# Local attention, six layers on one core: weighing the values ahead of projecting new ones on TensorE, and copying the new values out last on ScalarE

## The reference

```python
qkv = x @ Wqkv                      # x: tokens shifted by one in half of the channels
q, k, v = split(qkv)
q = rotary(l2norm(q) * qs);  k = rotary(l2norm(k) * ksc)
sim = einsum('bhwie,bhwje->bhwij', q, k_of_this_and_previous_window) * 8.0
sim = where(mask, -max, sim)        # windows of 32 tokens, each sees 64 keys
attn = softmax(sim)
out = einsum('bhwij,bhwje->bhwie', attn, v_of_this_and_previous_window)
x = out @ Wo + x
x = ffn(shift_tokens(x)) + x
```

## Time and profile before

| what | value |
|---|---|
| median of three runs | 4894.09 us |
| profiled execution | 4860.85 us, span 4859.0 us |
| the six layers | from about 1619 us to 4859 us of the span |
| steps of one tile | 32 in a layer, 192 in all, plus three draining steps in a layer |
| TensorE busy, whole span | 91% |
| VectorE, ScalarE, GpSimd busy | 76%, 57%, 45% |

### The profile page before, as it was taken

How to read it: one execution, slowest core, us unless ns; L and a number is a source line. 1 busy time by engine, 2 the same in 40 slices (tenths; PEclk the granted TensorE clock), 3 DMA queues, 4 the chain that set the end, 5 groups by cost and what they waited for, 6 DMA issues and landing times. The chain is left out here.

```text
span 4859.0 us, 169452 instructions
## 1 busy us (share of the span) xinstructions
PE 4413.6 (91%) x75386; PEld 2749.0 (57%) x75386; DVE 3699.8 (76%) x4213; ACT 2755.6 (57%) x3767; POOL 2167.2 (45%) x1739
## 2 busy tenths in 40 slices
PE   7959997767998699999999999999999999999998
PEld 5623333543333376756776577646775667657674
DVE  5668884137886588858987799868996888869885
ACT  4527775334777366545665566555665565556564
POOL 4340000330000466636664566636663666546661
PEclk9979998887999899999999999999999999999999
DMA  1021111112111211111111111111111111211110
GB/s 43 8 78 28 45 44 45 52 52 61 42 41 32 63 42 42 38 44 39 42 39 49 37 38 42 38 45 42 38 42 41 42 42 38 59 28 38 42 38 27
DMA packets 109872, 204.69 MB, mean 42 GB/s; under 512 B 30514, under 2 KB 58802, under 8 KB 107314
## 3 DMA queue, kind: packets, MB, share of 16 engines
q1 hardware_dynamic: 107096, 189.65, 15.1%
q0 software_dynamic: 2048, 4.20, 0.3%
HBM read 67.52 MB, written 22.81 MB: 19 GB/s over the span
## 5 line engine op out<-in xcount | busy, mean ns | idle before, releaser
L2056 POOL TENSOR_TENSOR part_of_layer<-part_of_layer,sine_of_layer 128x512 f32<-128x512 f32 x768 | 963.4, 1276 | 612.1 <-DVE sine_of_layer L1932 612.1
L2067 POOL TENSOR_TENSOR part_of_layer<-part_of_layer,inverse_of_layer 128x1024 f32<-128x1024 f32 x384 | 730.5, 1902 | 259.8 <-ACT inverse_of_layer L1818 244.7
L980 ACT ACTIVATE prob_of_ca<-ps 128x1024 f32<-128x1024 f32 (+3 forms) x768 | 593.2, 813 | 245.9 <-PE ps L858 170.3
L1929 DVE TENSOR_TENSOR part_of_layer<-ps,rope 128x1024 f32<-128x1024 f32 x384 | 466.0, 1213 | 35.7 <-ACT square_of_layer L1806 34.0
L1932 DVE TENSOR_TENSOR sine_of_layer<-ps,rope 128x1024 f32<-128x1024 f32 x384 | 464.7, 1210 | 0.0
L1849 ACT ACTIVATE values_of_layer<-ps 128x1024 f32<-128x1024 f32 x192 | 196.6, 1024 | 450.0 <-PE ps L1692 450.0
L876 PE MATMUL ps<-keys_of_ca,queries_of_ca 64*128 64x512 bf16 (+3 forms) x1536 | 326.1, 342 | 117.4 <-DVE top_of_ca L1013 59.7
L1711 PEld LDWEIGHTS ps<-prob_t_of_layer,mixed_of_layer 64*64 64x64 f32 x12288 | 340.1, 134 | 161.2 <-issue 157.9
L1718 PE MATMUL ps<-heads_out_of_layer,wo 128*128 128x128 f32 x3072 | 413.1, 278 | 11.7 <-ACT heads_out_of_layer L1838 10.3
L1968 DVE TENSOR_REDUCE total_of_layer<-prob_of_layer 128x16 f32<-128x1024 f32 x192 | 234.2, 1220 | 232.8 <-ACT prob_of_layer L1842 232.8
L1618 PE MATMUL ps<-qkv,shifted 128*128 128x512 f32 x768 | 382.2, 620 | 25.0 <-POOL values_of_layer L2070 19.9
(11 more groups left out here) (238 smaller groups left out, 8774.8 us busy)
## 6 DMA issues: line engine op xcount, KB each, us to landing
mixed_of_layer<-values_of_layer SPq DMA_DIRECT2D x636, 128.0 KB
mixed_of_layer<-values_of_layer SPq DMA_DIRECT2D x264, 64.0 KB
queries_of_ca<-q_parts SPq DMA_DIRECT2D x384, 32.0 KB
keys_of_ca<-k_parts SPq DMA_DIRECT2D x384, 32.0 KB
qkv<-in_qkv SPq DMA_DIRECT2D x6, 1536.0 KB, 6.4
q_parts<-parts_of_ci SPq DMA_DIRECT2D x16, 384.0 KB, 2.5
k_parts<-parts_of_ci SPq DMA_DIRECT2D x16, 384.0 KB, 2.6
rope<-in_rope SPq DMA_DIRECT2D x6, 1024.0 KB, 9.0
```

What stands on the lines that cost most here:

```text
L980: nc.scalar.activation(prob[:, i % 2, 2 * two:2 * two + 2, j:], ps[:, 2 * two:2 * two + 2, j:], ACT.Exp, scale=scale).then_inc(raised, 1)
L1929: nc.vector.tensor_tensor(part[:, t % 2, side], by_head(slot), table(2 * side, t), ALU.mult).then_inc(parts, 1)
L2056: nc.gpsimd.tensor_tensor(out, out, sine[:, side, :, (1 - to) * half:(2 - to) * half], ALU.add).then_inc(rotated, 1)
L2067: nc.gpsimd.tensor_tensor(part[:, t % 2, side], part[:, t % 2, side], by, ALU.mult).then_inc(scaled, 1)
```

## The change

In TensorE's list `weigh` of tile n-2 is called before `make_v` of tile n; in ScalarE's list `out_v` of tile n moves from before `raise_p` to behind `out_o`. Nothing is added or removed, and no wait is edited: each function takes its waits along.

```diff
@@ TensorE
                     steps((make_next_q, 0), (make_k, 0), (turn_q, 1), (project, 3), (turn_k, 1), (turn_last_p, 2),
-                          (project_rest, 3), (turn_other_p, 2), (last(lambda: turn(1)), 2), (score, 1), (last(lambda: turn(0)), 1), (make_v, 0), (weigh, 2),
+                          (project_rest, 3), (turn_other_p, 2), (last(lambda: turn(1)), 2), (score, 1), (last(lambda: turn(0)), 1), (weigh, 2), (make_v, 0),
                           (last(lambda: turn(2)), 2), (last(lambda: back(0)), 2))
@@ ScalarE
                     steps((square_next_q, 0), (square_k, 0), (out_q, 1), (out_k, 1), (out_p, 2), (last(lambda: square_of(1)), 2), (invert, 0),
-                          (out_v, 0), (raise_p, 1), (last(lambda: square_of(0)), 1), (out_o, 2), (last(lambda: norm_invert(0)), 1), (shift_low, 4))
+                          (raise_p, 1), (last(lambda: square_of(0)), 1), (out_o, 2), (out_v, 0), (last(lambda: norm_invert(0)), 1), (shift_low, 4))
```

## The result

The changed kernel takes **5351.85 us** (median of 4 runs, 5320.29 to 5367.73) where the kernel before takes 4893.99 us (4 runs): a ratio of 1.0926, 95% interval 1.0886 to 1.0966. The profiled execution took 5346.37 us, 485.5 us more than the profiled one of before. The forecast of 5157 us had the sign, and its range ended at 5235 us: too low by 195 us of 458.

The account below looks back on a forecast made before the run. TensorE was taken to bound the step: 8.38 + 5.13 + 1.87 us plus 0.10 us for other gaps, 15.48 us against 14.06. Over 180 steps, with step 32, 263 us more: 5157 us, ends 5089 (widened to 5075) and 5235 us.

Parts of the forecast that it names:

- The block ends: Gaps inside weigh stand where TensorE passes into the next fetched block of 256 instructions, which isn't there yet.
- Point 1: TensorE from the step's start to the start of score: unchanged at 8.38 us.
- Point 2: score and weigh together: 3.42 us of work, 5.13 us with the fetch; weigh's wait for VectorE's key reading costs nothing.
- Point 3: make_v on TensorE: 1.87 us as before, now with the next make_q behind it.
- the sum: Step of 15.48 us, 1.42 us over 14.06; 256 us in 180 steps, 263 us with step 32.
- Point 4: raise_p on ScalarE can start some 0.15 us earlier, worth nothing because TensorE has the longer loop.
- Point 5: out_v ends 16.5 us in, 1.1 us into the next step; turn_q, SyncE's DMAs and square_q stay covered.
- Point 6: In step 32, turn_q of tile 31 waits for make_v and out_v: 1.26 us more per layer, 7.6 us.
- The second case: Rival: the block is there in time, only weigh's wait moves; 14.2 us a step, 4929 us, 0.7% slower; chance 8%.
- The faster case: Rival: fetch runs far enough ahead, weigh loses its gaps; step 13.76 us, 4840 us; chance 3%.

Follow-up runs that it names:

- e4: Changed kernel with make_v's four matmuls done twice, once unused between score and weigh, once behind weigh: 5200.07 us, ratio 1.0672.
- e5: Changed kernel with the last four pairs of heads left out of weigh, 128 instructions instead of 256: 4962.29 us, ratio 1.0153.
- e3: Changed kernel with two of make_v's four matmuls put back between score and weigh: 5031.87 us, ratio 1.0324.
- e6: Kernel before with out_v behind out_o on ScalarE, but shift_low ahead of raise_p and the last tile's values copied out first: 4884.58 us, ratio 0.9993.
- e2: Kernel before with only ScalarE's half of the change, out_v behind raise_p and out_o: 4894.56 us, ratio 1.0046.
- e7: Kernel before with an added wait in weigh of tile n-2 for raise_p of tile n-1: 5683.02 us, ratio 1.1614.
- e1: Kernel before with only TensorE's half of the change, weigh ahead of make_v: 5574.55 us, ratio 1.1432.

## Why the prediction was right and wrong, point by point

**The block ends: right.** Gaps of 0.8 to 2.4 us, 1.5 on average from one weight load to the next, in 185 of 192 steps; e4 and e5 show that it is the spacing and the place of the block ends. With TensorE's instructions of the trace counted one by one, its semaphore instructions among them, all 185 gaps stand at a multiple of 256 from each other, to one instruction; so do the 26 of the kernel before and the 86 of e5. From the start of a block in `score` to the first instruction of the next one, in `weigh`, passed 3.5 us on average (1.1 us until the instruction packet started, 1.1 us for the packet, 1.4 us more until that instruction ran); in the two thirds of the steps where no other block end came just before, 3.39 us; step 32 of the kernel before had given 3.4 us on average over the six layers. One reading of the prediction was off without harm: the four transposes of step 32 are 8 instructions, four loads and four matmuls, and not 16.

```profile
3684.08 0.42 PEld L1738 LDWEIGHTS ps<-sb_ident,shifted 128*128 128x128 f32 x4
```

**Point 1, `make_q` to `score` 8.38 us: right** (8.37 us in the step shown).

**Point 2, the pair in 5.13 us: a little low.** 1.71 + 3.74 = 5.45 us. Step 32 of the kernel before doesn't have what a third of the steps have now, a block end that follows closely on another one; there the next block took 3.85 us to come. Another part is `weigh` itself at half clock. The wait for VectorE is there as worked out, 1.71 - 1.42 = 0.3 us, and costs nothing, since the gap ends later: e3 takes it away and gets back only what the spacing gives.

**Point 3, `make_v` 1.87 us as before: wrong, and this is the step that failed.** 2.64 us, and `make_q` behind it 0.09 us more. The prediction kept the granted clock at 1.00 in these steps, because the windows of before have 1.00 right through gaps of 1.3 us. But that was a small sample: in the ordinary steps of before only five gaps were of 0.9 to 1.7 us, and half clock followed none of them. In those of the changed kernel it followed 11 of 44 gaps of 0.9 to 1.3 us, 42 of 79 up to 1.7 us, 28 of 41 up to 2.1 us and 11 of 14 longer ones. The kernel before had a sign of it too: half clock fell into the 3 us behind `weigh` in step 32 of five of the six layers, the step that the 5.13 us were taken from (other idle time stands near it there). In layer 3:

```profile
3685.90:3690.00 4.10, 2.31 (x117) 2.20 (x118) 4.00 (x7) 2.60 (x3) 0.00 (x0) 1.00 0.01 4
3690.00:3693.50 3.50, 3.50 (x19) 3.50 (x19) 1.63 (x3) 0.41 (x2) 1.04 (x1) 0.53 0.02 5
```

The fall was named as what would make the forecast wrong, but given no chance and no price. Its price is an estimate: 474 - 65 = 409 us more at half clock, of which at most half, **204 us**, is lost. Some of it lies over idle time and costs nothing; but 280 us of it lie in `make_v` and 40 in `make_q`, dense work (`make_v` takes 3.75 us where the clock is at half throughout, 1.95 us where it is at full), so at least 160 us are lost. Without it 252 to 296 us are left of the 456 us that the layers take longer; the sum had 263.

**Point 4, nothing from `raise_p`: right** (e6).

**Point 5, `out_v` later and covered: right for the changed kernel, wrong for its half.** In the slower step `square_q` has its idle time back. With TensorE's order of before, e2, it has none, and in every fourth step it starts late.

**Point 6, step 32: right.** `turn_q` of tile 31 in layer 3, which answers to the earlier trace rows:

```profile
4010.41 1.94 PE L1692 MATMUL ps<-qkv,shifted 128*64 128x512 f32 x8
4013.56 1.06 PE L1639 MATMUL ps<-sb_ident,part_of_layer 128*128 128x128 f32 x8 [1.22 <-ACT values_of_layer L1849]
```

4013.56 - 4010.41 = 3.15 us behind `make_v`'s start, 3.13 forecast.

**The rivals.** The second case, the block there in time, had the skill's sentence for it, in the Trainium skill, page "Runtime: NRT & Kernel Launch", section "Instruction fetch mechanics", that crossing a block's end is mostly hidden; the runs go against it wherever two dense runs follow each other. The faster case needed 185 gaps not to be there.

## What to carry to other kernels

A TensorE program of many tiny matmuls can be bound by its own instruction fetch: look for idle time called "issue" inside a run of equal instructions, count to the next, and if it is 256 or a multiple, treat a few long matmuls between two dense runs as the cover they are. Don't move them out for the sake of a dependency that already has slack. And price idle time on TensorE twice: once for itself, once for the half clock that can follow it; here the second was 160 to 204 us beside 252 to 296 us for all the rest.

## What the hardware showed that I had not expected

The half clock doesn't need long idle times. Gaps of 0.9 us a step left it at 115 us in the layers (e3), 1.5 us at 474 us, 2.3 us at 910 us (e7), though TensorE was busy 91% of the time in the changed kernel's steps. The length of the gap isn't all: e1 has the changed kernel's gaps, 185 of 1.5 us, and longer waits beside them, yet only 371 us. And whether a gap brings half clock more easily because others came in the steps before it is not shown by any run.

A waiting TensorE can hold up its own fetch. In e7 the gaps that stayed inside `weigh` begin long after the block before was entered. One of layer 2: the block ends in `score` at 3340.57, itself late, and `weigh` waits until 3344.98; the next block is wanted and missing until 3349.24.

```profile
3340.57 0.14 PEld L1679 LDWEIGHTS ps<-keys_of_layer,queries_of_layer 64*32 64x32 f32 x5 [0.46 <-issue]
...
3344.98 0.24 PEld L1713 LDWEIGHTS ps<-prob_t_of_layer,mixed_of_layer 64*64 64x64 f32 x8 [3.12 <-issue]
3349.24 0.19 PEld L1713 LDWEIGHTS ps<-prob_t_of_layer,mixed_of_layer 64*64 64x64 f32 x3 [2.44 <-issue]
```

The DMA view shows no instruction packet between 3340.6 and 3346.2 us, and one from 3346.2 to 3349.3:

```profile
q8 instruction: 1, 0.02, 2.7%
```

8.7 us passed from one block to the next, over twice what a fetch needs, and its packet didn't start until the wait was over. The same holds for 31 of 34 late blocks of e7: the packet started 1.0 to 2.1 us after `weigh` began, and some 4.6 to 6.6 us after the block before was entered. In the blocks that were in time it started about 1 us after that entry, nearly always during the wait. Most of the late ones (28) are those whose block end followed on another one within 4 us; of the 123 blocks whose block end came over 5 us after the one before, 3 were late. That the wait holds up the asking is my reading, since the profile shows packets and not requests. Why it should hold up the one and not the other stays open; no run tells it apart.
